# Row maxima handed out in two halves of a unit's queries, one unit ahead

## What is computed

```python
scores = einsum('bhsd,bhtd->bhst', Q, K) / sqrt(8)
scores = where(causal, scores, -inf)
attn   = softmax(scores, axis=-1)
out    = einsum('bhst,bhtd->bhsd', attn, V)
```

## Time and profile before

| | |
|---|---|
| runs | 848.53, 849.88 and 850.32 us, median 849.88 us |
| profiled execution | 844.29 us, of which the trace spans 842.5 us |
| TensorE clock granted, mean | 0.898 |
| busy in the span | PE 688.3, DVE 588.4, ACT 441.8, POOL 313.4 us |

### The profile page before, as it was taken

The page is one execution under the profiler, slowest core; times in us unless marked ns, Lnnn a source line. Parts: engine busy times, 40 slices in busy tenths (PEclk is TensorE's granted clock), DMA queues, the critical chain, the costliest instruction groups (busy, mean ns, idle before and its releaser), DMA issues.

```text
span 842.5 us, 18794 instructions
## 1 busy us (share of the span) xinstructions
PE 688.3 (82%) x5544; PEld 362.3 (43%) x5545; DVE 588.4 (70%) x1443; ACT 441.8 (52%) x840; POOL 313.4 (37%) x512
## 2 busy tenths in 40 slices
PE   5859999899989888898889898988769947899840
PEld 2343333333433333343333333432259937898730
DVE  6959788888898977689888789894416731223266
ACT  1340366766646555555556664656736713565524
POOL 3871222232131245412116523124723465444551
PEclk9985599999989988898989999899969977999985
DMA  8784423111010111101002011000167745687924
GB/s 304 252 276 149 142 68 109 45 46 32 15 47 2 46 52 34 55 9 45 18 30 68 28 48 46 1 2 16 33 167 203 212 120 147 172 225 210 294 86 117
DMA packets 68038, 83.67 MB, mean 99 GB/s; under 512 B 9314, under 2 KB 45672, under 8 KB 67824
## 3 DMA queue, kind: packets, MB, share of 16 engines
q1 hardware_dynamic: 63600, 74.04, 29.6%
q0 software_dynamic: 4352, 8.53, 2.9%
HBM read 55.77 MB, written 26.90 MB: 98 GB/s over the span
## 4 chain that ended last, share of the span: by engine, by line
PE 48%; DVE 23%; issue 11%; SPq 7%; ACT 4%; DMA 2%; another core or an unknown queue 2%; POOL 1%; DVEq 0%; ACTq 0%; POOLq 0%
PE banks L711 14%; DVE mx L1121 13%; PE banks L668 9%; PE banks L693 6%; PE banks L784 4%; PE banks L663 4%; PE banks L773 4%; PE banks L720 2%; SPq L567 2%; ACT region L829 2%; SPq L568 2%; SPq L561 1%; DMA region<-pairs 1%; DVE w_sb L908 1%
## 5 line engine op out<-in xcount | busy, mean ns | idle before, releaser
L1121 DVE TENSOR_REDUCE mx<-banks 128x1 f32<-128x512 f32 (+3 forms) x640 | 365.6, 630 | 57.9 <-PE banks L668 50.5
L829 ACT ACTIVATE region<-banks 128x1024 f32<-128x1024 f32 (+3 forms) x256 | 200.7, 837 | 147.2 <-PE banks L693 144.6
L668 PE MATMUL banks<-region 64*128 64x512 bf16 (+3 forms) x768 | 201.1, 360 | 12.7 <-DVE mx L1121 11.1
L693 PE MATMUL banks<-region 64*128 64x512 bf16 (+3 forms) x768 | 134.6, 347 | 17.6 <-ACT region L829 9.8
L711 PE MATMUL banks<-region 128*32 128x512 f32 (+3 forms) x1024 | 122.7, 553 | 3.2 <-POOL region L1365 3.1
L829 ACT ACTIVATE cs_sb<-banks 128x1024 f32<-128x1024 f32 (+2 forms) x128 | 90.3, 760 | 62.5 <-PE banks L693 57.7
L663 PE MATMUL banks<-mask_sb,half_sb 64*128 64x128 bf16 (+1 forms) x384 | 87.5, 255 | 36.3 <-DVE mx L1121 24.7
L1375 POOL DMA_INDIRECT results<-region,dest x72 | 71.9, 998 | 106.1 <-DVE region L1248 72.2
L1365 POOL TENSOR_SCALAR_AFFINE_SELECT region<-region 128x256 f32<-128x256 f32 x160 | 64.8, 412 | 98.0 <-ACT region L829 95.5
L784 PE MATMUL banks<-region,w1e 128*128 128x128 f32 x576 | 83.4, 292 | 19.2 <-ACT region L855 14.4
L1242 DVE TENSOR_TENSOR region<-banks,w1e 128x128 f32<-128x128 f32 x72 | 20.9, 291 | 111.8 <-PE banks L773 65.8
(11 more groups left out here) (176 smaller groups left out, 703.8 us busy)
## 6 DMA issues: line engine op xcount, KB each, us to landing
w1e<-in_w SPq DMA_DIRECT2D x72, 322.0 KB
region<-stack SPq DMA_DIRECT2D x128, 112.0 KB
stack<-x_sb SPq DMA_DIRECT2D x16, 384.0 KB, 3.3
region<-pairs SPq DMA_DIRECT2D x72, 66.0 KB
stack<-x_sb SPq DMA_DIRECT2D x16, 256.0 KB, 3.7
region<-results SPq DMA_DIRECT2D x8, 512.0 KB, 4.7
xT_sb<-in_xT SPq DMA_DIRECT2D x4, 512.0 KB, 12.2
stack<-fill SPq DMA_DIRECT2D x2, 1024.0 KB, 10.3
```

The costliest lines, as they stand in the source:

```text
L668: last = mm(ring[:, bank, m * n:(m + 1) * n], qst[rows, v % NG, slot_, sb_ * P:(sb_ + 1) * P], kst[rows, v % NG, slot_, t0:t0 + n], start= ...
L693: last = mm(score[:, slot_, par, 0:n], kst[rows, u % NG, slot_, j * P:(j + 1) * P], qst[rows, u % NG, slot_, s0:s0 + n], start=True, stop= ...
L829: nc.scalar.activation(probs[i % 6][:, :, 0:n], score[:, i % 2, :, 0:n], ACT.Exp, scale=SCALE).then_inc(exp_done, 1)
L1121: read(v.tensor_reduce(dst, src, AX.X, ALU.max, negate=True))
```

## The change

The maxima of a unit are handed out in two halves c = 0, 1 of 512 queries. Each half has its own SPLIT (four operations on half as many columns), MT, copy and two MROWS DMAs with half the bytes each, and its own semaphores `mrows[c]`; QK waits for half 0 before step 0 and for half 1 before step 4. The pass now leads by one unit: steps 0 to 11 of unit u carry the 40 items of unit u+1, by the new quota 4, 3, 3, 1, 4, 5, 4, 4, 5, 3, 2, 2. SPLIT of half 0 of unit u+1 stands at step 4, MT and MROWS at step 5; SPLIT of half 1 at step 11, MT and MROWS at step 0 of unit u+1 itself. In the prologue only the 40 items of unit 0 remain, with half 0 handed out among them; no items are left from unit 15 on. `qst` has the two halves apart, so `load_unit` issues two DMAs of half the rows' length for each one of the queries: 12 instead of 8. The routing matmuls "LG" and "RK" take two ring slots each instead of one, and LG's first half stands one step earlier.

```diff
-A_LEAD, A_END = 7, 6
+A_HALF = sum(1 for it in A_ITEMS if it[1] < CH // P)
...
-    ev += [("A", 0, i) for i in range(NA)] + [("SPLIT", 0)]
-    lead = NB - A_LEAD
-    ev += [("A", 1, i) for i in range(quota[lead - 1])]
-    ev.insert(len(ev) - quota[lead - 1] // 2, ("MT", 0))
-    ev.insert(len(ev) - quota[lead - 1] // 2, ("MROWS", 0))
+    first = next(k for k in range(NB) if quota[k] >= A_HALF)
+    ev += [("A", 0, i) for i in range(A_HALF)] + [("SPLIT", 0, 0)]
+    middle = (A_HALF + NA) // 2
+    ev += [("A", 0, i) for i in range(A_HALF, middle)] + [("MT", 0, 0), ("MROWS", 0, 0)]
+    ev += [("A", 0, i) for i in range(middle, NA)] + [("SPLIT", 0, 1)]
...
-            if k >= A_LEAD:
-                v, i = u + 2, k - A_LEAD
-            else:
-                v, i = u + 1, k + NB - A_LEAD
+            if u + 1 < NU:
+                items = [("A", u + 1, n) for n in range(quota[k - 1] if k else 0, quota[k])]
...
-            if k == A_END and u + 1 < NU:
-                ev.append(("SPLIT", u + 1))
+            if u + 1 < NU and k in (first, NB - 1):
+                ev.append(("SPLIT", u + 1, int(k == NB - 1)))
...
-            if k == A_END + 1 and u + 1 < NU:
-                ev += [("MT", u + 1), ("MROWS", u + 1)]
+            if k == first + 1 and u + 1 < NU:
+                ev += [("MT", u + 1, 0), ("MROWS", u + 1, 0)]
+            if k == 0:
+                ev += [("MT", u, 1), ("MROWS", u, 1)]
...
+                            if w_ == 0:
+                                for c in range(2):
+                                    sp.dma_start(qst[rows, g, c, slot_, :],
+                                                 src[:, :, :, c * CH:(c + 1) * CH].rearrange("o z r n -> (o z) r n")
+                                                 ).then_inc(dma_unit[g], 16)
...
-                    if k == 0 and slot_ == 0:
+                    if j == 0 and slot_ == 0:
-                        pe.wait_ge(mrows[u % 2], at(32 * (u // 2 + 1), 32 * NG // 2))
+                        pe.wait_ge(mrows[c][u % 2], at(32 * (u // 2 + 1), 32 * NG // 2))
```

More of the change, by code:

```diff
@@ L107, in a_quota @@
 def a_quota():
-    steps = [k % NB for k in range(A_LEAD, NB + A_END + 1)]
-    work = [B_STEPS[k][3] for k in steps]
+    work = [st[3] for st in B_STEPS]
     return [NA * sum(work[:i + 1]) // sum(work) for i in range(len(work))]
@@ L413, in build @@
         msplit = sem("msplit")
-        mrows = [sem(f"mrows{i}") for i in range(2)]
+        mrows = [[sem(f"mrows{c}_{i}") for i in range(2)] for c in range(2)]
         qk_done = sem("qk_done")
@@ L495, in load_unit @@
             def load_unit(b, g):
-                for w_, dst in ((0, qst), (1, kst)):
+                for w_ in range(2):
                     for par in (0, 1):
@@ L667, in visit @@
                     for m, slot_ in enumerate(slots):
-                        last = mm(ring[:, bank, m * n:(m + 1) * n], qst[rows, v % NG, slot_, sb_ * P:(sb_ + 1) * P],
+                        last = mm(ring[:, bank, m * n:(m + 1) * n], qst[rows, v % NG, sb_ // 4, slot_, sb_ % 4 * P:(sb_ % 4 + 1) * P],
                                   kst[rows, v % NG, slot_, t0:t0 + n], start=(m == 0 and not is_masked),
@@ L693, in visit @@
                         last = mm(score[:, slot_, par, 0:n], kst[rows, u % NG, slot_, j * P:(j + 1) * P],
-                                  qst[rows, u % NG, slot_, s0:s0 + n], start=True, stop=True)
+                                  qst[rows, u % NG, c, slot_, s0 - c * CH:s0 - c * CH + n], start=True, stop=True)
                     last.then_inc(qk_done, 1)
@@ L723, in visit @@
                 elif kind == "LG":
[L724 to L730, removed]
+                    bt, c = e[1:]
+                    pe.wait_ge(ring_read, at(RING_OF[("T2", bt, c)] + 1, RING_BATCH))
+                    for t in range(4):
+                        last = mm(ring[:, bank, t * E:(t + 1) * E], aT[:, c, t * P:(t + 1) * P], wg_sb[:, :],
+                                  start=(t == 0), stop=True, skip_group_check=True)
                     last.then_inc(ring_full, 1)
@@ L734, in visit @@
                     pe.wait_ge(top_mask, at(e[1] + 1, 1))
[L735 to L738, removed]
+                    mm(ring[:, bank, 0:BT * E], before_sb[:, e[2], :], rt[:, 4, :, :], start=True, stop=True
+                       ).then_inc(ring_full, 1)
                 elif kind in ("T1", "WO", "T2"):
@@ L1127, in visit @@
                 elif kind == "MT":
-                    read(v.tensor_copy(mparts[:, e[1] % 2, :], ring[0:GH * 3 * BT, bank, 0:P // 2].bitcast(BF16)))
+                    read(v.tensor_copy(mparts[:, e[1] % 2, e[2], :], ring[0:HALF_ROWS, bank, 0:P // 2].bitcast(BF16)))
                 elif kind == "OT":
@@ L1142, in visit @@
                 elif kind == "LG":
-                    read(v.tensor_tensor(logits[:, :, :],
-                                         ring[:, bank, 0:BT * E].rearrange("p (t e) -> p t e", t=BT),
-                                         bg_sb[:, :].unsqueeze(1).broadcast_to([P, BT, E]), ALU.add))
+                    c = e[2]
+                    read(v.tensor_tensor(logits[:, 4 * c:4 * c + 4, :],
+                                         ring[:, bank, 0:4 * E].rearrange("p (t e) -> p t e", t=4),
+                                         bg_sb[:, :].unsqueeze(1).broadcast_to([P, 4, E]), ALU.add))
                 elif kind == "RK":
-                    read(v.tensor_copy(ranks[:, :, :, :], ring[:, bank, 0:2 * BT * E].rearrange(
-                        "p (k t e) -> p k t e", k=2, t=BT)))
+                    read(v.tensor_copy(ranks[:, e[2], :, :], ring[:, bank, 0:BT * E].rearrange(
+                        "p (t e) -> p t e", t=BT)))
                 elif kind in ROUTE_STEPS:
```

70 lines of the change are left out of this document (41 added, 29 removed).

## The result

The median of four runs fell from 849.2 to 831.57 us. The ratio of the two kernels run beside each other is 0.9875, 95% interval 0.9827 to 0.9924, which is 10.6 us of 849.88; a second series gave 0.9879 (0.9842 to 0.9916). The two medians alone would give 0.979, outside the first interval; in the second series, with more runs, they are 835.67 and 846.47 us, 0.987, so I go by the ratios. The change makes the kernel faster, by 0.8 to 1.7%, and by more than the 4.7 us forecast. The profiled execution takes 828.04 us, with a span of 825.9.

What follows compares the result with a forecast made beforehand. No one engine was taken to bound the kernel: PE and DVE wait for each other through ring and program order. Terms -8.4 + 3.1 + 3.7 - 1.0 - 2.1 = -4.7 us gave 845.2 us, range 838 to 856.

Steps and rivals of the forecast that it cites:

- the likeliest case: Whole kernel: the summed forecast holds, with 842 to 848 us, chance 0.38.
- Term 1: Prologue: 15 items leave it before the first QK, -8.4 us.
- Term 2: SP's queue in the prologue: four more DMA issues delay ACT's wait and pass A, +3.1 us (1.5 to 3.3).
- Term 3: Unit 14: steps 7 to 11 now carry 16 items, +3.7 us (+1.7 to +5).
- Term 4: Unit 15: scatters start earlier, easing POOL's backlog and ACT's idling before step 4, -1.0 us (-2.9 to +1.3).
- Term 5: Units 0 to 13: items in another phase, one reduction saved against a new MT wait, -2.1 us (-10 to +6).
- a sign of being wrong: PE, each unit: idle over 0.5 us before the MT line L675, ended by POOL, would show the forecast wrong.
- the counted reduction: Units 0 to 13: one DVE reduction less as small items move to narrow steps, -0.6 us a unit.
- The late rows of half 1: QK of step 4 waits for row writes, PE stands 0.5 to 1.1 us each unit, 852 to 861; chance 0.26.
- The units gain more: Small items fit free beside narrow steps, -7 to -10 us, or SP's issues cost 1.5; 836 to 842; chance 0.18.
- No gain: Units 0 to 13: steps merely swap burdens, 0 to +2 us, result 847.3 to 849.5; chance 0.18.

Runs made afterwards that it cites:

- second pair of profiles: Kernel before and changed kernel each profiled once more without edits; kernel before 842.62 us, changed kernel ratio 0.9879.
- SPLIT ahead of the mask: Changed kernel with SPLIT of half 1 ahead of the mask of step 0's second half on POOL; ratio 0.982 to the kernel before.
- old lead: Changed kernel's two halves kept, items back at the lead of 1.42 units; ratio 1.0149 to the kernel before.
- load by ACT: Changed kernel with the twelve DMAs that load unit 0 issued by ACT instead of SP; ratio 0.9826 to the kernel before.
- other shares: Changed kernel with the 40 items shared otherwise among the steps; ratios to the kernel before: weighted by VectorE's work 1.0245, nearly flat 0.9854, a few items moved 0.9819.
- the late rows: Changed kernel with MT and MROWS of half 1 at step 2 of the unit instead of step 0; 927.33 us in one run.
- three edits: Changed kernel with a few items moved between steps, unit 0's load issued by ACT, and SPLIT of half 1 before the mask; ratio 0.9801 to the kernel before.
- flat and moved shares: Changed kernel with items shared nearly evenly among steps, or with one item each moved out of steps 4, 5, 7 and 8; ratios 0.9854 and 0.9819.
- the combinations: Changed kernel with load and SPLIT edits; these plus moved items; the same with the changed kernel's share in units 5, 9, 13; ratios 0.982, 0.9801, 0.9763.
- load and SPLIT together: Changed kernel with unit 0's load issued by ACT and SPLIT of half 1 ahead of the mask; ratio 0.982 to the kernel before.

## Why the prediction came out as it did

The direction was right and the whole lies in the range, but the gain was more than twice the forecast, and the likeliest case's own range (842 to 848, or 0.991 to 0.998 of the median before) does not hold the measured 0.9875.

- **Term 1** (15 items leave the prologue, -8.4): right. From the start of pass A to the first QK PE now takes 21.5 us instead of 30.5, -9.0.
- **Term 2** (four more issues, +3.1): right in place, and near in price. The four issues hold SP 3.07 us. ACT's copies and pass A come 3.87 us later, but of that 1.07 was there before the load, in ACT's first rounding:

```profile
18.36 1.04 ACT L807 CAST x_sb<-w_sb 128x1024 bf16<-128x1024 f32 x1 [16.29 <-DVE w_sb L908]
```

```profile
19.43 1.05 ACT L814 CAST x_sb<-w_sb 128x1024 bf16<-128x1024 f32 x1 [17.36 <-DVE w_sb L915]
```

  The first line is before, the second after. Counted from it the copies come 2.80 us later, and in the second pair of profiles 2.33. The Trainium skill, DMA: Bandwidth & Descriptors, Anatomy of one DMA, gives about 50 ns for a dispatch, on GpSimd's path. It was rightly kept out of the sum: on SP's queue an issue at half the row length held SP 6.51 / 8 = 0.81 and 6.24 / 8 = 0.78 us.
- **Term 3** (unit 14, +3.7): +1.9 and +4.0 in two profiles, right within its ends.
- **Term 4** (unit 15, -1.0): -1.9, inside its ends. ACT's idle time before step 4 fell from 2.94 us to 1.43, the place that the term named.
- **Term 5** (units 0 to 13, -2.1) is the step that failed, by its size: -8.3. It set one reduction, -0.6, against a wait of +0.45, so -0.15 a unit; a plain unit lost 0.67. The wait came where it was described, on PE ahead of MT, and was longer, 0.62 us in plain units instead of 0.3, and over 0.5 is what the prediction had named as a sign of being wrong; but it was worth 0.14 (SPLIT ahead of the mask). That PE and VectorE share slack through the ring is my reading of it. The items' new place was worth an estimated -0.81 with the waits out (old lead, SPLIT ahead of the mask).

Where the 0.67 us lie, by the time in us from the first exponential of a step to that of the next, in unit 2:

| step | 0 | 1 | 2 | 3 | 4 | 5 | 6 | 7 | 8 | 9 | 10 | 11 |
|---|---|---|---|---|---|---|---|---|---|---|---|---|
| before | 1.82 | 2.22 | 2.03 | 2.13 | 1.83 | 2.56 | 2.42 | 3.98 | 2.80 | 2.53 | 2.71 | 1.38 |
| after | 1.83 | 2.40 | 1.76 | 2.30 | 1.82 | 2.28 | 3.11 | 3.46 | 2.65 | 2.96 | 1.70 | 1.48 |
| change in the number of items that the step before carries | +1 | -1 | 0 | +1 | 0 | -1 | +1 | -1 | 0 | +1 | -1 | 0 |

Step 7 fell by 0.52, near the 0.6 of the counted reduction, but step 6 grew by 0.69: the new quota gives one item less to step 6 and one more to step 5, and the sum had only the first. What won is step 10, -1.01. Before, four items of the first half, masked and 512 keys wide, were reduced beside its narrow exponential; now it has one item less. ACT at steps 10 and 11 of unit 1, before and after:

```profile
147.04 1.08 ACT L829 ACTIVATE region<-banks 128x512 f32<-128x512 f32 x2 [1.01 <-PE banks L693]
149.75 0.66 ACT L829 ACTIVATE cs_sb<-banks 128x256 f32<-128x256 f32 x2 [1.63 <-PE banks L693]
```

```profile
141.93 1.09 ACT L836 ACTIVATE region<-banks 128x512 f32<-128x512 f32 x2 [1.45 <-PE banks L704]
143.63 0.74 ACT L836 ACTIVATE cs_sb<-banks 128x256 f32<-128x256 f32 x2 [0.61 <-PE banks L704]
```

Steps 0 to 4, where the small items stand now, grew by 0.08 in all. No run keeps the number of items of each step and moves only the small ones, so how much belongs to the number and how much to the kind of the items is not shown.

- **Rivals.** The late rows of half 1 did not come, by an estimated 0.85 us. "The units gain more" gave 836 to 842, which holds the result, and was right that small items fit beside narrow steps; but it looked for the gain between steps 7 and 8, and it came at step 10, so its number is in part luck. It deserved more than 0.18. The upper end of "No gain" should be 849.3 (849.88 - 2.6 + 2.0), not 849.5.
- **The range.** 0.9875 of 849.88 is 839.3 us, 1.3 above the lower end of the range: its width took in what term 5 missed. The 0.2% that the prediction took as the least that can be told was too fine, with intervals of 0.4 to 0.5% to either side.

What is shown: the prologue's terms (stretches of two profiles, load by ACT), that the order of the items and the place of the hand-out change a plain unit (old lead, other shares), the small worth of the MT wait. Not settled: what makes up the -5.2 us of units 4 to 13, since these units change by 1 to 4 us between two executions.

## What to carry to other kernels

Where two engines are each nearly full and coupled by a small ring, price a move of work by the stretches with the longest steps on both sides of the move, not by one step: here single items in other steps changed a unit by 1.3 us one way and 0.7 the other, while an idle 0.62 us on the critical engine was worth 0.14. Count the items of every step, not only of the step that seems overfull. A queue of DMA issues in a prologue is work on a path like any other, and an idle engine can take it over. And before a difference in one stretch is explained, profile the unchanged kernel twice.

## What was not expected of the hardware

In unit 7, unit 11 or both in nearly all profiles (in the first one before it was unit 6, with the late rows there was none) ACT, and at times DVE, stand for some us with no releaser among this core's engines. POOL may still run scatters then, as at 441.12 and 443.05 us below. With three edits, in unit 11, by the list of who waited for whom:

```profile
ACT region L850 <- remote: 5.5, 1, 5.5
...
DVE rden L1155 <- remote: 3.4, 1, 3.4
```

PE then waits 3.24 us for DVE, and its next matmuls take 0.60 us instead of 0.38, by its timeline:

```profile
442.15 0.38 PE L700 MATMUL banks<-region 64*128 64x512 bf16 x1
445.77 0.60 PE L674 MATMUL banks<-region 64*128 64x512 bf16 x1 [3.24 <-DVE attn L1157]
```

0.60 against 0.38 is the 1.2 against the 2.4 GHz level: the granted clock is 1.00 from 440.00 to 443.50 us and 0.50 from 445.77 to 449.00. Such waits of ACT add up to 3.1 and 5.0 us in the two profiles before, 0.9 and 3.5 in the two after, 7.1 with the old lead, and 6.8 to 13.1 with the flat and moved shares and the combinations. Their cause was not found. Two of the profiles with more than 6 us, the old lead and load and SPLIT together, have neither the flat nor the moved share, so those alone do not bring them about. They may be one part of why the units with routing scatter.
